# A cross-attention and mixture-of-experts layer in fp32: the first tiles of two experts moved into the seam between the stages, and keys and values projected as three fp32r products of parts

## The chip, the core and the metric

The kernel runs on one core of a Trainium2 chip. The metric is the device time of one execution in microseconds (us), from the first to the last instruction of the core and what lies around it. Three runs of the kernel before took 1197.14, 1199.79 and 1202.40 us, a median of 1199.79 us. The execution that was profiled took 1202.42 us, of which the trace's span is 1200.6 us.

## The reference

There are 16 batches of 256 tokens with 256 features, 16 heads of 16 features in the attention, and 8 experts with an inner width of 1024, of which each token goes to 2.

```python
x = x + tanh(g_xattn) * attention(layernorm(x), ctx, ctx)     # 16 heads, projections with biases
h = layernorm(x)
bids = sigmoid(h @ conf_w.T + conf_b) * wealth                # 8 experts
top_bids, selected = top_k(bids, 2)
combine = one_hot(selected) * softmax(top_bids)
x = x + tanh(g_ffn) * sum_e combine_e * (silu(h @ gate_e.T) * (h @ up_e.T)) @ down_e.T
```

The wealth of the experts differs, so the routing is skewed. With the inputs that are timed, the experts receive 1, 1, 272, 1, 3820, 1, 3 and 4093 of the 8192 assignments.

## The kernel before

The kernel has two stages, each written out engine by engine, with semaphores between the engines. Every engine executes its own list in order: SyncE (SP) and GpSimd (POOL) issue the DMAs, TensorE (PE) multiplies and transposes, ScalarE (ACT) and VectorE (DVE) read the PSUM results.

**The attention stage** (`attention_stage`) handles one batch after another. An iteration, the function `body` of each engine, holds work of several batches at once: the scores and the weighted values of batch b (`score`, `weigh`), the values and the row maxima of batch b+1 (`project_v`, `max_scores`), the layer norm and the projections of queries and keys for batch b+2 (`norm_x`, `project_k`, `project_q`), the output projection and the second layer norm of batch b-1, and the routing of batch b-2 (`first_choice`, `second_choice`, `positions`, `scatter`). The scatter writes each token's normalized row, with its weights and its number, to the region of each chosen expert in a DRAM tensor, `dispatched`. Batches 2 to 13 run in a hardware loop of two iterations a turn; iterations 0, 1, 14 and 15 are written out.

In an iteration GpSimd executes this list: the four small operations of the layer norm's scale for batch b+2 (`scale_x`, L1069 to L1072), the split of the dense keys into a rounded part and a rest (`split`, L1089 and L1091), the scale of the second layer norm, the split of the queries, four indirect DMAs (`scatter`, L1098), and the addition of the output bias to x (`add_bias`, L1081). ScalarE begins an iteration with `norm_x` of batch b+2, which waits for `scale_x`, and executes the exponentials of batch b (L703) behind it. TensorE's second `score` of the iteration writes the PSUM tile that the first exponential must have read. Keys and values are projected by plain fp32 matmuls of the context and the weights (L463 and L478).

**The seam.** After iteration 15 the last batch goes through a chain with one engine after another: heads turned, output projection, residual and second layer norm, routing, scatter. Then the rows behind each expert's last row are padded (`pad_experts`, from SP's and ACT's queues). All engines wait in `attention_over` until everything has landed. Only then are the rows of expert 0 loaded (`load_rows`, L1248). The weights of expert 0 are loaded at the start of the kernel, those of experts 1 and 2 behind `attention_over` (L87).

**The expert stage** (`expert_stage`) goes through the experts 0 to 7. The first tile of each has 128 rows and is computed in fp32 (`first`: gate and up at L1330, transposes at L1341, down at L1350). It is computed for every expert, whatever its count. Meanwhile ScalarE and VectorE split the expert's weights into a rounded fp32r part and a rest. Tiles behind it have 256 rows and consist of fp32r products of parts (`rest`, L1287 to L1301). Their number is read from the counts: 1 for expert 2, 15 for expert 4, 16 for expert 7, none for the others. Each tile's result is added to the output by indirect DMAs (L1511, L1519).

Of the kernel before, what the change touches and what calls it, by code (L numbers as in the profile page):

```python
# [21 lines left out]
P = 128  # L22
# [14 lines left out]
STAGES = 3  # L37
ROW = 272
COMB = D
# [18 lines left out]
def build_program(nc, x, ctxT, wq, wk, wv, wo, bq, bk, bv, bo, confT, conf_b, wealth, g_attn, g_ffn,  # L58
# [3 lines left out]
    with ExitStack() as keep:  # L62
# [8 lines left out]
        stage = sb(keep, "stage", [P, WCOLS])  # L71
# [3 lines left out]
        tiles = sb(keep, "tiles", [P, EXPERTS], i32)  # L75

# [3 lines left out]
        s_padded = [sem("expert0_padded"), sem("others_padded")]  # L80
# [3 lines left out]
        def load_third(eng, e, n, to):  # L84

            of = (gate_T, up_T, down_T)[n][e]
            eng.dma_start(to[:, n * third:(n + 1) * third], of).then_inc(s_stage[e % STAGES][n], 16)  # L87

        *attention, attention_over = attention_stage(nc, sb, sem, load_third, stage, disp, out, x, ctxT, wq, wk, wv, wo,
                        bq, bk, bv, bo, confT, conf_b, wealth, g_attn, g_ffn, ident, tri,  # L90
                        expert_row, expert_no, token_no, ones_at, pick_rows, pad_rows, idn, pads, s_padded, counts, tiles)
        experts = expert_stage(nc, sb, sem, load_third, disp, out, idn, tiles, stage, s_stage, s_hi, s_split, s_padded, attention_over)
        block = keep.enter_context(nc.Block())

        @block.sync
        def _(sp):
            attention[0](sp)
            experts[0](sp)

        @block.tensor  # L100
        def _(pe):
            attention[1](pe)
            experts[1](pe)

        @block.scalar
        def _(act):
            attention[2](act)
            experts[2](act)

        @block.vector  # L110
        def _(dve):
            attention[3](dve)
            experts[3](dve)

        @block.gpsimd
        def _(pool):
            attention[4](pool)
            experts[4](pool)
# [18 lines left out]
def attention_stage(nc, sb_in, sem, load_third, stage, disp, out, x, ctxT, wq, wk, wv, wo,  # L137
                    bq, bk, bv, bo, confT, conf_b, wealth, g_attn, g_ffn, ident, tri,
                    expert_row, expert_no, token_no, ones_at, pick_rows, pad_rows, idn, pads, s_padded, counts, tiles):
    with ExitStack() as own:  # L140
# [3 lines left out]
        x_all = sb("x_all", [P, BATCHES, QT, D])  # L144
# [3 lines left out]
        wv_s = sb("wv_s", [P, HC, D])  # L148
        wo_s = sb("wo_s", [P, HC, D])
        bq_s = sb("bq_s", [P, HC])  # L150
# [23 lines left out]
        xn = sb("xn", [P, QT, D])  # L174
        xT = sb("xT", [P, HC, SEQ])
        dense = {what: sb(f"{what}_dense", [P, HC, SEQ]) for what in "QK"}
        high = {what: sb(f"{what}_high", [P, HC, SEQ], f32r) for what in "QK"}
        rest = {what: sb(f"{what}_rest", [P, HC, SEQ], f32r) for what in "QK"}
        q = [sb(f"queries{i}", [P, HPAIRS, SEQ], f32r) for i in range(2)]
        k = [sb(f"keys{i}", [P, HPAIRS, SEQ], f32r) for i in range(2)]  # L180

        picks = {what: sb(f"picks_{what}", [P, QT, P], f32r) for what in ("Q high", "Q rest", "K high", "K rest")}
# [4 lines left out]
        probs = [sb(f"probs{i}", [P, HPG, QT, SEQ]) for i in range(2)]  # L187
# [25 lines left out]
        w2 = sb("w2", [P, QT])  # L213
# [1394 lines left out]
```

## Time and profile before

| what | us |
|---|---|
| median of three runs | 1199.79 (1197.14 to 1202.40) |
| the profiled execution | 1202.42 |
| its span | 1200.6 |
| before the steady iterations of the attention | 0 to 102.5 |
| iterations 2 to 13 | 102.5 to 431.0 |
| iterations 14 and 15 | 431.0 to 476.6 |
| the seam, to the first matmul of expert 0 | 476.6 to 514.7 |
| first tiles of experts 0 and 1 | 514.7 to 542.3 |
| the rest of the experts | 542.3 to 1200.6 |

In a row of the timeline stand the start, the duration, the engine, the line, the operation, the output and its inputs, and in brackets how long the engine had been idle before it and what ended that. An fp32 matmul shows as two records. TensorE's granted clock (PEclk) is given as a share of 2.4 GHz; it is either 1.00 or 0.50, and a value between them is a mean over a stretch that had both. Busy time of TensorE includes the modelled ends of its matmuls.

### The profile page before, as it was taken

To read this page: it belongs to the slowest core of one execution; us is meant where nothing else is said; L and a number is where in the kernel's file an instruction comes from. 1 tells how busy PE (TensorE), PEld (TensorE's weight loads), DVE (VectorE), ACT (ScalarE), POOL (GpSimd) and SP (SyncE) were. 2 spreads that over 40 slices of the span, in tenths; PEclk is the share of its full clock that TensorE was granted. 3 is DMA by queue.
4 is the path that set the end of the run, shared out by engine and by line. 5 is a ranking of instruction groups with operands and counts; after the bars stand their busy time and mean duration, and the time that the engine had idled before them with its cause. 6 is when DMAs were issued, how large, how long until landed. Compare 5 with 4: busy or idle time off the path is not lost. (4 is left out here: it accounts for less than half of the span.)

```text
span 1200.6 us, 24032 instructions
## 1 busy us (share of the span) xinstructions
PE 1091.6 (91%) x8213; PEld 896.2 (75%) x8213; DVE 668.0 (56%) x1588; ACT 555.3 (46%) x891; POOL 315.6 (26%) x366
## 2 busy tenths in 40 slices
PE   5789999999999988289899999999989999999994
PEld 4456666666666655247599999999849999999994
DVE  2546777777777774365644444444564444444442
ACT  3456676666676664155533333333453333333331
POOL 2122444444343332311311122112221122112111
PEclk8899999999999997589999999999999999999998
DMA  8100111111111101384621121112141122112111
GB/s 297 52 15 24 39 37 44 48 46 37 37 37 37 44 30 48 121 317 164 220 56 32 22 36 32 28 30 36 31 140 28 22 36 36 31 23 36 32 26 23
DMA packets 48025, 72.85 MB, mean 61 GB/s; under 512 B 6256, under 2 KB 42864, under 8 KB 44912
## 3 DMA queue, kind: packets, MB, share of 16 engines
q0 software_dynamic: 16896, 43.53, 14.2%
q1 hardware_dynamic: 30000, 27.68, 7.8%
q10 hardware_dynamic: 1088, 1.11, 0.3%
q8 instruction: 23, 0.38, 0.1%
q14 instruction: 18, 0.15, 0.0%
HBM read 47.14 MB, written 24.90 MB: 60 GB/s over the span
## 5 line engine op out<-in xcount | busy, mean ns | idle before, releaser
L1519 POOL DMA_INDIRECT out<-y,token x64 | 104.6, 1634 | 473.1 <-DVE y L1453 364.1
L1379 ACT ACTIVATE silu<-gate 128x512 f32<-128x512 f32 x128 | 76.5, 597 | 277.4 <-PE up L1287 277.4
L1299 PE MATMUL down<-w_split,h_hi 128*128 128x512 f32 x512 | 185.9, 398 | 0.0
L901 DVE TENSOR_REDUCE max_neg<-maxps 128x4 f32<-128x1024 f32 x128 | 156.4, 1222 | 52.8 <-PE maxps L510 51.1
L1287 PE MATMUL gate<-x_hi,w_split 128*128 128x256 f32 x1024 | 184.5, 282 | 0.0
L1287 PE MATMUL up<-x_hi,w_split 128*128 128x256 f32 x1024 | 183.8, 281 | 0.0
L1444 DVE TENSOR_TENSOR h<-silu,up 128x512 f32<-128x512 f32 x128 | 88.0, 688 | 171.4 <-ACT silu L1379 171.4
L703 ACT ACTIVATE probs<-scores 128x1024 f32<-128x1024 f32 x124 | 127.8, 1030 | 60.5 <-PE scores L535 60.5
L1287 PEld LDWEIGHTS gate<-x_hi,w_split 128*128 128x128 f32 x1024 | 148.8, 188 | 3.0
L1287 PEld LDWEIGHTS up<-x_hi,w_split 128*128 128x128 f32 x1024 | 147.8, 188 | 0.0
L1301 PE MATMUL down<-w_split,h_lo 128*128 128x256 f32 x512 | 144.2, 282 | 0.0
L1446 DVE TENSOR_TENSOR h_lo<-h,h_hi 128x512 fp32r<-128x512 f32 x128 | 88.6, 692 | 89.3 <-ACT h_hi L1382 89.3
L1382 ACT ACTIVATE h_hi<-h 128x512 fp32r<-128x512 f32 x128 | 80.8, 632 | 96.5 <-DVE h L1444 96.5
L1299 PEld LDWEIGHTS down<-w_split,h_hi 128*128 128x128 f32 x512 | 96.3, 188 | 17.4
L1287 PE MATMUL up<-x_lo,w_split 128*128 128x256 f32 x512 | 102.8, 282 | 0.0
L1287 PE MATMUL gate<-x_lo,w_split 128*128 128x256 f32 x512 | 102.6, 282 | 0.0
L1301 PEld LDWEIGHTS down<-w_split,h_lo 128*128 128x128 f32 x512 | 96.6, 189 | 0.0
L1287 PEld LDWEIGHTS up<-x_lo,w_split 128*128 128x128 f32 x512 | 78.7, 189 | 0.0
L1287 PEld LDWEIGHTS gate<-x_lo,w_split 128*128 128x128 f32 x512 | 78.0, 188 | 0.0
L546 PE MATMUL pv<-probs,values 128*32 128x256 f32 x1024 | 71.1, 397 | 1.4 <-ACT probs L703 1.4
L535 PE MATMUL scores<-queries,keys 64*128 64x256 f32 x496 | 60.0, 321 | 12.6 <-ACT probs L703 9.0
L510 PE MATMUL maxps<-keys,queries 48*128 48x256 f32 x512 | 60.8, 316 | 11.1 <-DVE max_neg L901 8.9
(164 smaller groups left out, 1756.3 us busy)
## 6 DMA issues: line engine op xcount, KB each, us to landing
xg<-dispatched SPq DMA_DIRECT2D x41, 272.0 KB, 2.8
stage<-gate_T POOLq DMA_DIRECT2D x8, 1024.0 KB, 7.5
stage<-up_T POOLq DMA_DIRECT2D x8, 1024.0 KB, 9.4
stage<-down_T POOLq DMA_DIRECT2D x8, 1024.0 KB, 12.0
x_all<-x SPq DMA_DIRECT2D x16, 256.0 KB, 6.3
ctxT<-ctxT SPq DMA_DIRECT2D x16, 256.0 KB, 2.7
out<-x_all SPq DMA_DIRECT2D x16, 256.0 KB, 2.1
out<-y,token POOLq DMA_INDIRECT x72, 3.8
```

Of the source, the lines that this page charges most:

```text
L510: last = mm(maxps[:, u, t, :], q[par][r, pair, t * P:(t + 1) * P], k[par][r, pair, :], start=True, stop=True)
L546: last = mm(pv[j * SLOT:(j + 1) * SLOT, 0:SEQ], v[par][:, t, g * HPG + j, :], probs[g % 2][:, j, t, :], start=t == 0, stop=t == QT - 1)
L703: nc.scalar.activation(probs[g % 2][:, at:at + HPP].rearrange("p u t s -> p (u t) s"), home(b, pair), ACT.Exp).then_inc(s["unit_read"], 1)
L901: V.tensor_reduce(to, maxps[:], AX.X, ALU.max, negate=True).then_inc(s["max_taken"], 1)
L1287: last = mm(bank[:, i, :], weights(w, mat)[:, c, cols], r[:, c, :], start=m == 0, stop=m == len(terms) - 1)
L1299: mm(down[t][:].rearrange("p (n d) -> p n d", n=2), h_hi[:, i, rows], split[:, :, cols], start=i == 0, stop=False, skip_group_check=True)
L1301: last = mm(down[t][:, 0:D], h_lo[:, i, rows], hi[:, cols], start=False, stop=i == IC - 1, skip_group_check=True)
L1379: nc.scalar.activation(silu[pair % 2][:], gate[pair % 2][:], ACT.Silu).then_inc(s_silu, 1)
L1382: nc.scalar.activation(h_hi[:, 2 * pair:2 * pair + 2, :], h[pair % 2][:], ACT.Copy).then_inc(s_hhi, 1)
L1444: V.tensor_tensor(h[pair % 2][:], silu[pair % 2][:], up[pair % 2][:], ALU.mult).then_inc(s_made, 1)
L1446: V.tensor_tensor(h_lo[:, 2 * pair:2 * pair + 2, :], h[pair % 2][:], h_hi[:, 2 * pair:2 * pair + 2, :].bitcast(fp32), ALU.subtract).then_i ...
L1519: pool.indirect_dma_start(out, bass.IndirectOffsetOnAxis(token[:, t:t + 1], axis=0), y[:, t, :], None, compute_op=ALU.add).then_inc(s_adde ...
```

## The change

The change has four parts.

**Parts of keys and values.** From iteration 2 on, the keys of batch b+2 and the values of batch b+1 are projected by `project_k_in_parts` and `project_v_in_parts`: the context and the weights are each split into a rounded fp32r part and a rest, and three of the four products of parts are summed, 12 fp32r matmuls in place of 4 fp32 ones. VectorE splits the weights once, before iteration 0 (`split_weights`); TensorE waits for it before iteration 0. GpSimd splits the context of batch b+3 at the end of each iteration (`split_ctx`), twice in iteration 1.

**Early tiles.** The first tiles of experts 0 and 1 are computed in the seam, interleaved with the last batch's chain on TensorE, ScalarE and VectorE. Their rows come from batches 0 to 12 alone. Where an expert has under 128 rows by then, as both have here, its later rows are placed behind row 128 (`space_early_experts`), and zero rows stand between; these are stored from SP's queue before iteration 0, and GpSimd waits for them there (`first_rows_padded`). The main loop then runs over experts 2 to 7, and last over tiles of experts 0 and 1 behind the first, of which there are none with these inputs.

**Loads.** The weights of expert 1 are loaded during the attention into a buffer of their own, those of expert 2 ahead of the last batch's scatter, those of experts 3 and 4 behind it. Weights of experts 0 and 1 are loaded once more in the main loop.

**Pads.** Those of experts 0 to 3 are stored from SP's queue, those of 4 to 7 from GpSimd's, behind the last scatter. Experts 4 to 7 are waited for only ahead of expert 4's rows.

```diff
+            def project_k_in_parts(b, par, use):
+                pe.wait_ge(s["ctx_split"], b - 2)
+                use.free(pe, "K")
+                terms = three_terms(w_high["k"], w_rest["k"], c_high[par], c_rest[par])
+                for o in range(HC):
+                    for n, (l, r, c) in enumerate(terms):
+                        last = mm(use.bank("K")[:, o, :], l[:, c, o * P:(o + 1) * P], r[:, c, :], start=n == 0, stop=n == len(terms) - 1)
+                last.then_inc(s["misc_written"], 1)
...
+            def split_ctx(c, par, use):
+
+                alone.wait_ge(s["ctx_loaded"], c * 16 + 16)
+                use.written(alone, "V")
+                G.tensor_copy(c_high[par][:], cT[par][:]).then_inc(s["ctx_high_made"], 1)
+                alone.wait_ge(s["ctx_high_made"], c - 2)
+                G.tensor_tensor(c_rest[par][:], cT[par][:], c_high[par][:].bitcast(fp32), ALU.subtract).then_inc(s["ctx_split"], 1)
...
                     scatter(b - 2, par)
                 if ahead:
                     add_bias(b + 2)
+                if isinstance(b, int) and b == 1:
+                    split_ctx(3, 1, use)
+                if ahead and not is_first(b):
+                    split_ctx(b + 3, 1 - par, use)
...
             add_bias(0)
             add_bias(1)
+            pool.wait_ge(s["first_rows_padded"], 16 * EARLY)
...
+                if pair >= 6:
+                    split_weights(pair - 6, "kv"[pair - 6], (wk_s, wv_s)[pair - 6])
             read_maxima(0, PRO1)
...
             sp.dma_start(out[TOKENS:], pads[:, 0:D]).then_inc(s["pads_stored"], 16)
+            for e in range(EARLY):
+                sp.dma_start(disp[e * REGION:e * REGION + FIRST], pads[:]).then_inc(s["first_rows_padded"], 16)
...
+            turn_last_heads()
+            pe.wait_ge(s["unit_read"], handed["units"])
+            turn_rows(16 * EARLY, EARLY)
+            turn_last_normed()
+            early_product(0, 0, 0)
+            project_last_out()
+            early_product(0, 0, 1)
+            early_product(0, 1, 0)
+            early_product(0, 1, 1)
+            turn_last_x2()
+            early_flip(0, 0)
+            last_logits()
...
+            scatter_next_to_last()
+            pool.wait_ge(s["x2_stored"], 16 * BATCHES)
+            load_weights(EARLY)
+            scatter_last()
...
+        ORDER = [*range(EARLY, EXPERTS), *range(EARLY)]
```

GpSimd's list around the end of an iteration in the loop, before. `rstd` and `shift` are the four operations of `scale_x` for the next iteration; the rows named ISA set registers for waits.

```order
L1098 DMA dispatched<-row,posi 34816x272 x4
L1081 ISA
L1081 TENSOR_TENSOR x_all<-x_all,bo_s 128x512
L131 ISA
L1069 TENSOR_SCALAR rstd<-mv 128x2
L131 ISA
L1070 TENSOR_TENSOR rstd<-rstd,minus_half 128x2
```

And GpSimd's list at the same place now.

```order
L1183 DMA dispatched<-row,posi 34816x272 x4
L1158 ISA
L1158 TENSOR_TENSOR x_all<-x_all,bo_s 128x512
L131 ISA x2
L1164 CAST ctx_high<-ctxT 128x512
L131 ISA
L1166 TENSOR_TENSOR ctx_rest<-ctxT,ctx_high 128x512
L131 ISA
L1146 TENSOR_SCALAR rstd<-mv 128x2
L131 ISA
L1147 TENSOR_TENSOR rstd<-rstd,minus_half 128x2
```

The two operations of `split_ctx` stand between the bias and the scale on which the next iteration's first instruction of ScalarE waits.

TensorE's list in the seam before, from the transposes of the last heads (L556) to the count (L691) and the first rows of expert 0 (L1276).

```order
L556 MATMUL misc<-idn,oS 128x128 x8
L451 MATMUL misc<-idn,on 128x128 x4
L568 MATMUL misc<-wo_s,oT 128x256 x4
L588 MATMUL misc<-m,before 128x8
L591 MATMUL misc<-macc,ones 128x8
L588 MATMUL misc<-m,before 128x8
L590 MATMUL misc<-m,ones 128x8
L591 MATMUL misc<-macc,ones 128x8
L451 MATMUL misc<-idn,row 128x128 x4
L580 MATMUL misc<-conf_s,x2T 128x8 x4
```

And TensorE's list now, from the same transposes to the logits (L614). `x_early` holds the turned rows of experts 0 and 1.

```order
L590 MATMUL misc<-idn,oS 128x128 x8
L1399 MATMUL turned<-idn,xg 128x128 x4
L464 MATMUL misc<-idn,on 128x128 x4
L1498 MATMUL gate<-stage,x_early 128x512 x2
L602 MATMUL misc<-wo_s,oT 128x256 x4
L622 MATMUL misc<-m,before 128x8
L625 MATMUL misc<-macc,ones 128x8
L622 MATMUL misc<-m,before 128x8
L624 MATMUL misc<-m,ones 128x8
L625 MATMUL misc<-macc,ones 128x8
L1498 MATMUL up<-stage,x_early 128x512 x2
L1498 MATMUL gate<-stage,x_early 128x512 x2
```

Two matmuls of expert 0's tile stand ahead of the last output projection, and six more stand between the ranks and the transposes of the last normalized rows. The other matmuls of the two tiles follow in the same way, between the logits and the first rows of expert 2.

## Rows read from the trace of the kernel before

**Rows 1.** Stretches: length, busy time (instructions) of five engines, granted clock, DMA, GB/s.

```profile
102.50:431.00 328.50, 306.17 (x2728) 214.23 (x2724) 245.80 (x684) 221.34 (x348) 140.40 (x204) 1.00 0.12 40
476.60:514.70 38.10, 10.50 (x39) 8.39 (x39) 13.26 (x80) 6.02 (x12) 12.52 (x19) 0.58 0.40 141
514.70:542.30 27.60, 26.89 (x88) 15.27 (x88) 18.97 (x27) 17.69 (x26) 3.32 (x4) 0.90 0.80 317
```

**Rows 2.** Timeline of TensorE, a steady iteration: second scores, keys, second scores.

```profile
327.94 0.50 PE L535 MATMUL scores<-queries,keys 64*128 64x256 f32 x4
...
353.38 1.99 PE L463 MATMUL misc<-ctxT,wk_s 128*128 128x256 f32 x8
355.31 0.50 PE L535 MATMUL scores<-queries,keys 64*128 64x256 f32 x4
```

**Rows 3.** Timeline of TensorE, fp32r matmuls of 256 columns in a 256-row tile.

```profile
562.42 0.64 PE L1287 MATMUL up<-x_hi,w_split 128*128 128x256 f32 x4
562.89 0.40 PE L1287 MATMUL up<-x_lo,w_split 128*128 128x256 f32 x2
```

**Rows 4.** Timeline of GpSimd, from the split of the queries to the next scale.

```profile
341.64 0.61 POOL L1089 CAST Q_high<-Q_dense 128x512 fp32r<-128x512 f32 x1 [1.87 <-ACT Q_dense L739]
342.40 1.28 POOL L1091 TENSOR_TENSOR Q_rest<-Q_dense,Q_high 128x512 fp32r<-128x512 f32 x1 [0.15 <-POOL Q_high L1089]
...
348.76 1.28 POOL L1081 TENSOR_TENSOR x_all<-x_all,bo_s 128x512 f32 x1
350.27 0.23 POOL L1069 TENSOR_SCALAR rstd<-mv 128x2 f32<-128x2 f32 x1 [0.23 <-DVE mv L859]
```

**Rows 5.** Timeline of ScalarE, the start of the same iteration.

```profile
352.22 1.09 ACT L717 ACTIVATE xn<-x_all,shift,rstd 128x256 f32 x2 [2.11 <-POOL shift L1072]
353.22 1.00 ACT L703 ACTIVATE probs<-scores 128x1024 f32<-128x1024 f32 x1
```

**Rows 6.** Stretches as in rows 1: around falls of the clock, and a steady one.

```profile
445.00:452.00 7.00, 4.12 (x48) 2.59 (x52) 5.59 (x22) 5.19 (x8) 3.64 (x7) 0.98 0.14 50
588.60:592.00 3.40, 3.40 (x6) 1.35 (x5) 1.92 (x2) 0.00 (x0) 3.05 (x4) 0.55 1.02 429
325.80:332.70 6.90, 6.35 (x58) 4.48 (x57) 5.81 (x13) 5.76 (x11) 1.88 (x2) 1.00 0.00 0
```

**Rows 7.** Timeline of iteration 0, and GpSimd's at the start of iteration 2.

```profile
47.23 0.43 SPq L419 DMA_DIRECT2D out<-pads  x1
...
47.00 0.23 POOL L1069 TENSOR_SCALAR rstd<-mv 128x2 f32<-128x2 f32 x1 [18.53 <-DVE mv L859]
...
49.87 1.00 ACT L703 ACTIVATE probs<-scores 128x1024 f32<-128x1024 f32 x1
...
52.94 0.50 PE L535 MATMUL scores<-queries,keys 64*128 64x256 f32 x4
...
104.10 0.22 POOL L1069 TENSOR_SCALAR rstd<-mv 128x2 f32<-128x2 f32 x1 [5.83 <-DVE mv L859]
```

**Rows 8.** Timeline of the seam and the first tiles of experts 0 to 2.

```profile
478.88 3.68 PE L568 MATMUL misc<-wo_s,oT 128*128 128x256 f32 x8 [0.69 <-ACT oT L731]
...
487.94 1.11 PE L451 MATMUL misc<-idn,row 128*128 128x128 f32 x4 [4.92 <-ACT row L726]
...
495.63 1.28 ACT L833 ACT_TABLE_LOAD   x1
...
503.29 0.96 POOL L1098 DMA_INDIRECT dispatched<-row,posi  x1 [0.30 <-issue]
...
509.14 0.06 DVE L1479 MEMSET note<- 128x4 f32 x1 [9.38 <-DMA dispatched<-row,posi]
...
514.73 3.78 PE L1330 MATMUL gate<-stage,x_full 128*128 128x512 f32 x4 [1.69 <-DVE x_lo L1419]
...
529.91 1.96 PE L1330 MATMUL gate<-stage,x_full 128*128 128x512 f32 x4
...
542.40 1.89 PE L1330 MATMUL gate<-stage,x_full 128*128 128x512 f32 x4
```

More of the change, by code:

```diff
@@ L67, in sem @@
             return keep.enter_context(nc.semaphore(name))
-        stage = sb(keep, "stage", [P, WCOLS])
+        stage = [sb(keep, f"stage{i}", [P, WCOLS]) for i in range(EARLY)]
         idn = sb(keep, "idn", [P, P])
@@ L1186, in expert_stage @@
         s_first_added = sem("first_added")
+        s_own_hi = [sem(f"expert{e}_weights_hi") for e in range(EARLY)]
+        s_own_split = [[sem(f"expert{e}_weights_split{n}") for n in range(3)] for e in range(EARLY)]
         third = WCOLS // 3
@@ L1365, in first, with early_product @@
                 first_contract(e, 1, range(IC // 2)).then_inc(s_down, 1)
-            turn_rows(16)
+            def early_product(e, half, mat):
+                if mat == 0 and half == 0:
+                    pe.wait_ge(s_xhi, EARLY)
+                    for n in range(2):
+                        wait_stage(pe, e, n)
+                for c in range(HC):
+                    last = mm(early_bank((gate, up)[mat], e, half)[:].rearrange("p a b -> p (a b)"),
+                              x_early[:, c, e * FIRST:(e + 1) * FIRST],
+                              weights(stages[e], mat)[:, c, half * (INNER // 2):(half + 1) * (INNER // 2)],
+                              start=c == 0, stop=c == HC - 1)
+                if mat == 1:
+                    last.then_inc(s_pair, 2)
@@ new lines, in early_flip @@
+            def early_flip(e, half):
+                pe.wait_ge(s_made, e * PAIRS + (2 * half + 4))
+                if half == 1:
+                    pe.wait_ge(s_flipped, 2 * e + 1)
+                for i in range(IC // 2):
+                    last = nc.tensor.transpose(early_bank(gate, e, 0)[:].rearrange("p a b -> p (a b)")[:, i * P:(i + 1) * P],
+                                               h[half][:].rearrange("p a b -> p (a b)")[:, i * P:(i + 1) * P], idn[:])
+                last.then_inc(s_flip, 1)
@@ new lines, in early_contract @@
+            def early_contract(e, half, pieces):
+                wait_stage(pe, e, 2)
+                pe.wait_ge(s_flipped, 2 * e + half + 1)
+                w = weights(stages[e], 2)
+                for i in pieces:
+                    at = half * (IC // 2) + i
+                    last = mm(early_bank(up, e, 0)[:].rearrange("p a b -> p (a b)")[:, 0:D], hT[half][:, i, :], w[:, at, :],
+                              start=at == 0, stop=at == IC - 1)
+                return last
+            turn_last_heads()
@@ L1383, in rest, with round_part, before_rest @@
                 high_of_rows(n + 2)
+            def round_part(e, m, half, done):
+                wait_stage(act, e, m)
+                nc.scalar.activation(hi[:, part(m, half)], stages[e % STAGES][:, part(m, half)], ACT.Copy).then_inc(done, 1)
+            def before_rest(e, r):
+                if e < EARLY:
+                    act.wait_ge(s_down, r + EXPERTS)
+                    for m in range(3):
+                        act.wait_ge(s_split[m], 2 * splits_before(EXPERTS))
+                    for m, half in HALVES:
+                        round_part(e + EXPERTS, m, half, s_own_hi[e])
             def first(e, r, n):
@@ L1387, in round_weights @@
                     for m, half in halves:
[L1388 to L1389 removed]
+                        round_part(e, m, half, s_hi)
                 def first_silu(half):
```

466 lines of the change are left out of this document (307 added, 159 removed).

## Prediction

> **What bounds the kernel now.** I first cut the span into its stages [rows 1]. In the twelve steady iterations of the attention TensorE is busy for 306 of 328.5 us, in the first tiles of two experts for 26.9 of 27.6 us. In the seam it is busy for 10.5 of 38.1 us, at a mean clock of 0.58, while the last batch goes from engine to engine. So TensorE sets the time in the stages, and a chain of waits in the seam. Next I read the timeline where the change puts instructions. The second scores of an iteration come 27.37 us after those of the one before [rows 2]. Beside TensorE runs a second chain that is almost as long: GpSimd splits the queries, issues four scatters, adds the bias, computes the scale; then ScalarE normalizes x and does the first exponential, which TensorE's second scores wait for [rows 4, 5]. How much air that chain has decides what the first part of the change is worth.
>
> **Keys and values in parts.** The fp32 projection holds TensorE for 1.93 us, from 353.38 to 355.31 [rows 2]; values have the same shapes. An fp32r matmul of 256 columns takes 0.118 us, four of them 0.47 us from 562.42 to 562.89 [rows 3]; twelve take 1.42 us. Each projection gives back 0.5 us. There are 12 of keys and 13 of values; if TensorE alone decided, the gain would be 12.5 us.
>
> It does not decide. The split of a batch's context on GpSimd has the shapes of the split of the queries: 0.61 + 0.15 + 1.28 us, with the registers for its waits about 2.15 us [rows 4]. It stands between the bias and the scale. The air in front of the scale is 0.23 us (it waits for VectorE until 350.27) [rows 4]. The first exponential ends at 354.22 [rows 5], and TensorE's second scores start at 355.31 [rows 2], 1.09 us later, of which 0.06 us is the signal. Together that is 1.26 us of air, and 2.15 us is put in: the second scores come 0.9 us later than before. From there to the next projection of queries, and through GpSimd's list to the next scale, each step waits for the one before, and nothing in it gets shorter: both projections that do lie ahead of the second scores, where TensorE will now wait. So the iteration grows to 28.3 us, and the 1.0 us that it saves becomes part of a wait of 1.9 us. This holds at 11 starts of iterations (3 to 13): +9.9 us. At the start of iteration 2 GpSimd was idle for 5.83 us [rows 7], which holds both of its splits; iterations 2 and 14 therefore keep what they save, three projections, -1.5 us. Bounds for this term: -12.5 us (no wait) and 11 x 2.15 = +24 us (no air).
>
> VectorE's instructions may be held up while GpSimd computes. The splits fall beside VectorE's reading of the values; even 2 us there would be hidden, since TensorE waits for the exponential anyway. I take nothing.
>
> **The clock in these iterations.** TensorE's clock fell after 445 to 452, where it was busy for 4.12 of 7.00 us; in a steady iteration it was busy for 6.35 of 6.90 us around the second scores and stayed at 2.4 GHz [rows 6]. With the new wait (1.9 us, of which 0.16 us is covered by the modelled end of the last matmul) that place has 4.6 of 6.9 us. This is much nearer to the row that fell. I take a fall at every second of the 11 places. A fall costs at least half of a stretch like 588.6 to 592.0, 1.7 us [rows 6]: 5.5 x 1.7 = +9 us. Bounds: 0, and 11 falls of twice that length, +37 us.
>
> The Trainium skill (TensorE: Matmul & The Clock Gate, "Why this matters for your kernels") names only long idle gaps between bursts of matmuls as what brings the clock down. By that rule waits of 1.9 us would leave it up, the 9 us would be 0, and this is the first rival. The trace does not agree with it in full: in 445 to 452, before the fall, TensorE had no such gap and was busy for 4.12 of 7.00 us [rows 6].
>
> **Ahead of iteration 0.** GpSimd's scale of batch 2 starts at 47.00 [rows 7]. Now it waits for two stores of zero rows that SP issues behind `out<-pads`, at 47.23 [rows 7] and later by what the split of the weights on VectorE puts in front of the last maxima: a copy and a subtraction, about 1.2 us (GpSimd takes 1.28 us for such a subtraction alone [rows 4]). With the issue of two stores more and about 2 us to land (an estimate) this is 51.5, so +4.5 us. The first exponential ended at 50.87, and the second scores of iteration 0 started at 52.94 [rows 7], 2 us later; +2.6 us remain. Bounds 0 and +5.
>
> **The seam.** A first tile takes 12.49 us at 2.4 GHz, from 529.91 to 542.40 [rows 8]; two take 25 us. TensorE is idle in the seam for 27.6 us [rows 1], and its own 10.5 us get shorter when the clock stays up. The pieces stand where the chain is elsewhere. Two matmuls (1.7 us) go ahead of the output projection, which took 3.68 us while the clock fell [rows 8] and takes 2.0 us with it up; this is even. Six matmuls (5.2 us) fit into the 4.92 us before 487.94 [rows 8], since the projection ends sooner. ScalarE loads its table again ahead of the sigmoid and of the next silu; 1.28 us each [rows 8], of which about 0.6 us comes onto the chain. I expect the last scatter within 1 us of 503.29. It stands on GpSimd's queue behind 3.1 MB of expert 2's weights; at the 317 GB/s of 514.7 to 542.3 [rows 1] these take 10 us from about 493, so they end with the scatters. Half of the pads are no longer ahead of it all. So expert 2 starts where expert 0 did, at 514.73, in place of 542.40: -27.7 us. It also takes over expert 0's low clock, 15.2 us (514.73 to 529.91) in place of 12.5: +2.7 us. For the four late pads I take -1 us. Sum -26 us. Bounds: 0 (all of it at 1.2 GHz, 50 us of tiles in 38 us of seam) and -29.
>
> **The end.** Reading the two counts of experts 0 and 1 again, +0.5 us. Their second loads of weights, 6.3 MB, lie beside the 31 large tiles of experts 4 and 7: nothing. If that cover were gone, the rate above would make it 20 us.
>
> **The sum.** -1.5 + 9.9 + 9 + 2.6 - 26 + 0.5 = -5.5 us, so 1202.42 becomes 1196.9 for an execution like the profiled one. That one lies 2.6 us above the median of the three; against the median it is 1194.3, and I forecast 1194 us.
>
> **The rivals.**
> 1. *The clock stays up in the attention.* For it: 4.6 of 6.9 us is still a larger share than that of the stretch that fell. Against it: it is nearer to that one than to the steady one. The 9 us fall away: 1185 us.
> 2. *GpSimd's chain has more air than I count*, for instance because its list runs ahead, and TensorE keeps the 12.5 us. Then the sum is -12.5 + 2.6 - 26 + 0.5 = -35.4: 1164 us. Against it: the idle 2.11 us of ScalarE before it normalizes x show that it already waits for GpSimd [rows 5].
> 3. *The clock falls in nearly every iteration* (slower). The place is the wait ahead of the second scores; the price is 1.7 us for each fall and 3.4 us where the clock stays down for twice as long. Without falls the sum is -14.5 us, so it decides from 14.5 us on, nine single falls in eleven. With eleven falls of mean 2.6 us it is +29 - 14.5 = +14: 1214 us.
> 4. *The seam gives nothing back:* the clock is low through it as before, or the last scatter waits behind the weights. Then 20 of the 26 us are lost: 1214 us. For it: mean clock 0.58 now [rows 1]. Against it: TensorE is nearly always busy there afterwards.
>
> **How the numbers follow.** The forecast has 0.41, with its own range from 1187 to 1202; rival 1 has 0.17, rival 2 0.10, rival 3 0.17, rival 4 0.15. About 0.5%, 6 us, is what a measurement of this kernel can tell from no change. Faster than 1193.8: rivals 1 and 2, and under half of the forecast (0.18): 0.45. Slower than 1205.8: most of rivals 3 and 4: 0.28. Between them 0.27. The range from 1176 to 1213 leaves out rival 2 and the far half of 3 and 4.
>
> **What would show it.** The second scores 28.3 us apart, with GpSimd's context split directly before the scale and ScalarE waiting about 4 us for the scale; TensorE waiting about 1.8 us for the first exponential; stretches of clock 0.50 between 110 and 440. Expert 2's first matmul near 515 plus what came before. Wrong would be: a period under 27.4 us; no wait for the exponential; TensorE still busy with expert 1 when expert 2's rows have landed.

## The result, and the profile after

| | kernel before | changed kernel |
|---|---|---|
| median of its timed runs | 1201.25 us (1196.91 to 1204.61, 16 runs) | 1204.52 us (1200.85 to 1212.16, 16 runs) |
| span of the profiled execution | 1200.6 us | 1201.2 us |
| ratio | 1 | 1.0041, 95% interval 1.0023 to 1.0059 |

The change made the kernel 0.4% slower (medians 3.3 us apart); the forecast was 1194 us, 5.5 us less than before. Follow one instruction per place through both traces, and one sees where the difference arises. "Rest of the keys" is GpSimd's subtraction `K_rest` (L1091 before, L1176 now), which stands in each of the iterations 0 to 13:

| place | before | after | difference so far |
|---|---|---|---|
| rest of the keys, iteration 3 | 139.73 | 139.90 | +0.2 |
| rest of the keys, iteration 13 | 413.43 | 421.79 | +8.4 |
| expert 2's first matmul | 542.40 | 536.10 | -6.3 |
| expert 4's first matmul | 587.82 | 582.49 | -5.3 |
| end of the span | 1200.6 | 1201.2 | +0.6 |

So the attention lost 8.4 us, the seam gave back 14.7 us where 26 were forecast, experts 2 and 3 lost 1.0 us, and from expert 4's first tile on 5.9 us were lost, of which the prediction had 0.5 us. These are differences of two single executions: the one profiled before lies 1.2 us above its kernel's median, the one after 1.6 us below.

The stretches of the profile after (columns as in [rows 1]); the second row holds the new seam with the tiles of experts 0 and 1, the third what follows them:

```profile
102.50:431.00 328.50, 292.23 (x2734) 210.24 (x2734) 241.48 (x678) 214.33 (x337) 154.78 (x220) 1.00 0.12 42
478.00:517.20 39.20, 35.23 (x191) 22.12 (x183) 18.51 (x106) 17.36 (x29) 20.96 (x29) 1.00 0.53 189
517.20:537.00 19.80, 2.03 (x6) 1.21 (x6) 2.32 (x5) 2.85 (x5) 5.00 (x8) 0.60 0.99 365
```

The granted clock is 1.00 throughout the steady iterations, and also in the seam, where it was 0.58 [rows 1]. There TensorE is now busy for 35.23 of 39.20 us. But then it is busy for only 2.03 of 19.80 us, while the DMA engines are busy throughout (0.99).

The end of a steady iteration on GpSimd, ScalarE and TensorE, which answers to [rows 2, 4, 5]:

```profile
275.40 1.09 ACT L771 ACTIVATE xn<-x_all,shift,rstd 128x256 f32 x2 [3.97 <-POOL shift L1149]
...
299.52 0.61 POOL L1164 CAST ctx_high<-ctxT 128x512 fp32r<-128x512 f32 x1
300.28 1.28 POOL L1166 TENSOR_TENSOR ctx_rest<-ctxT,ctx_high 128x512 fp32r<-128x512 f32 x1
301.64 0.23 POOL L1146 TENSOR_SCALAR rstd<-mv 128x2 f32<-128x2 f32 x1
...
305.65 0.50 PE L569 MATMUL scores<-queries,keys 64*128 64x256 f32 x4 [1.35 <-ACT probs L757]
```

The scale of x directly follows the split of the context, with no idle time left ahead of it (0.23 us before). ScalarE waits 3.97 us for it (2.11 before), and TensorE 1.35 us for the first exponential. The period, that is the time from one iteration to the next, read at the rest of the keys from iteration 3 to 13, is 28.19 us (27.37 before).

The seam after on GpSimd, SP and TensorE:

```profile
500.83 0.60 POOL L91 DMA_DIRECT2D stage<-gate_T  x1
...
510.77 0.96 POOL L1183 DMA_INDIRECT dispatched<-row,posi  x1 [0.30 <-issue]
511.73 2.24 POOL L373 DMA_DIRECT2D dispatched<-pads  x3
...
516.67 1.25 POOL L91 DMA_DIRECT2D stage<-gate_T  x1
...
522.88 13.70 SPq L1365 DMA_DIRECT2D xg<-dispatched  x2
...
533.03 1.08 PE L1399 MATMUL turned<-idn,xg 128*128 128x128 f32 x4 [15.78 <-DMA xg<-dispatched]
536.10 3.75 PE L1456 MATMUL gate<-stage,x_full 128*128 128x512 f32 x4 [1.99 <-DVE x_lo L1644]
```

Two transfers are late. SP may issue expert 2's rows only when the last scatter has landed; that is at 522.88, 11.2 us after its issue ended (before: 509.11, 4.9 us). And TensorE turns (transposes) these rows, 272 KB, only 10.15 us after that (before 2.8 us, 509.11 to 511.93). It had been done with expert 1's tile since 517.25.

The large tiles, grouped, first before and then after (columns: count | busy us, mean ns of one):

```profile
L1299 PE MATMUL down<-w_split,h_hi 128*128 128x512 f32 x512 | 185.9, 398 | 0.0
L1287 PE MATMUL gate<-x_hi,w_split 128*128 128x256 f32 x1024 | 184.5, 282 | 0.0
```

```profile
L1422 PE MATMUL down<-w_split,h_hi 128*128 128x512 f32 x512 | 187.3, 403 | 0.0
L1410 PE MATMUL gate<-x_hi,w_split 128*128 128x256 f32 x1024 | 186.1, 284 | 0.0
```

The matmuls of both groups are a little slower at the same clock. From the turning of one tile's rows to the next it is 17.59 us and not 17.41; 31 times this is 5.6 us, nearly all of the 5.9.

### The profile page after: what moved, and what is told of

Read it like the earlier page. It is cut to its first block and busy times, and to the rows that moved or that the text cites. A ratio compares the mean times of both kernels' runs of the same rounds, so it can differ in the third digit from the quotient of the medians.

```text
span 1201.2 us, 24318 instructions
## 1 busy us (share of the span) xinstructions
PE 1083.5 (90%) x8310; PEld 897.7 (75%) x8310; DVE 654.5 (54%) x1575; ACT 545.3 (45%) x877; POOL 346.2 (29%) x404
## 5 line engine op out<-in xcount | busy, mean ns | idle before, releaser
L1410 PEld LDWEIGHTS up<-x_hi,w_split 128*128 128x128 f32 x1024 | 150.3, 191 | 0.0
L569 PEld LDWEIGHTS scores<-queries,keys 64*128 64x128 f32 x496 | 38.1, 189 | 58.2 <-ACT probs L757 36.3
```

Of the source, the lines that this page charges most:

```text
L569: last = mm(to[:, u * QT + t, :], k[par][r, pair, t * P:(t + 1) * P], q[par][r, pair, :], start=True, stop=True)
L1410: last = mm(bank[:, i, :], weights(w, mat)[:, c, cols], r[:, c, :], start=m == 0, stop=m == len(terms) - 1)
```

## The experiments

All ratios are against the kernel before, with 95% intervals; a time is the median of that kernel.

### The slower large tiles: e1, e5, e6, e10

e1 is the kernel before with the tiles of the experts where the changed kernel has them:

```diff
-        stages = [stage] + [sb(f"stage{i}", [P, WCOLS]) for i in range(1, STAGES)]
-        split = sb("w_split", [P, 2, WCOLS], f32r)
         xg = sb("xg", [P, TT, ROW])
+        x_early = sb("x_early", [P, HC, EARLY * FIRST])
...
+        h_hi = sb("h_hi", [P, IC, TILE], f32r)
+        split = sb("w_split", [P, 2, WCOLS], f32r)
+        h_lo = sb("h_lo", [P, IC, TILE], f32r)
```

> The kernel before with nothing changed but where the experts' tiles (rows, weights, their parts) lie in SBUF: the places of the changed kernel. Theory: the 256-row tiles of the changed kernel take 17.60 us and not 17.41 because of these places, so here their period becomes 17.60 and the time rises by 31 x 0.18 = 5.7 us, to about 1207. Rival: the slower tiles come from what the changed kernel does beside them (the second loads of weights, other instruction addresses, the power of what ran before); then the period stays 17.41 and the time 1201.

1206.06 us, ratio 1.0058 (1.0040 to 1.0076); from one large tile to the next 17.59 us. Its groups are those of the changed kernel:

```profile
L1303 PE MATMUL down<-w_split,h_hi 128*128 128x512 f32 x512 | 187.3, 403 | 0.0
L1291 PE MATMUL gate<-x_hi,w_split 128*128 128x256 f32 x1024 | 186.1, 284 | 0.0
```

So the places alone make the tiles as slow, without any work beside them. The next three keep the order of before and only insert unused gaps:

```diff
+        gap0 = sb("gap0", [P, 320])
         split = sb("w_split", [P, 2, WCOLS], f32r)
...
+        gap1 = sb("gap1", [P, 480])
         x_hi = sb("x_hi", [P, HC, TILE], f32r)
...
+        gap2 = sb("gap2", [P, 256])
         h_hi = sb("h_hi", [P, IC, TILE], f32r)
```

This is e5, with gaps of 320, 480 and 256 elements of 4 bytes; e6 has 96, 480 and 256, e10 only the first gap of 320. e11 to e16, further down, bring the changed kernel's tiles back to 17.41 us by such gaps.

> The kernel before with three unused gaps in the experts' SBUF, so that the parts of the weights, of the rows and of the hidden values start at the same remainder of 2048 bytes (896) as in the changed kernel (before: 1664, 1792 and 768), the order of the tiles being that of before. Theory: the slower large tile (17.60 us against 17.41) comes from these remainders; then the period is 17.60 and the time about 1206. Rival: it comes from the order, that is from the region of SBUF in which the parts lie; then the period stays 17.41 and the time 1201.

> The same gaps with other sizes, so that the parts of the weights, rows and hidden values all start at a multiple of 2048 bytes. If remainders matter, the period is another than 17.41 us, and an even start is at least as good as before: 17.2 to 17.4. If only the region matters, it stays 17.41 and the time 1201.

> The kernel before with one unused gap of 1280 bytes ahead of the parts of the weights: all parts move together, weights from remainder 1664 to 896 of 2048 (as in the changed kernel), rows from 1792 to 1024, hidden values from 768 to 0. Theory A: what counts is the distance of the two operands of a matmul (in both slow kernels weights, rows and hidden values had the same remainder); the distances stay as before, so 17.41 us and 1201. Theory B: the weights' own remainder counts: 17.60 us and 1206.

| | start in bytes, remainder of 2048: weights, rows, hidden | from tile to tile, us | time, ratio |
|---|---|---|---|
| before | 1664, 1792, 768 | 17.41 | 1 |
| e5 | 896, 896, 896 | 17.59 | 1208.02 us, 1.0070 (1.0054 to 1.0086) |
| e6 | 0, 0, 0 | 17.61 and 17.54 in turn | 1205.68 us, 1.0048 (1.0033 to 1.0062) |
| e10 | 896, 1024, 0 | 17.41 | 1200.46 us, 0.9999 (0.9985 to 1.0013) |

The order of the tiles does not matter (e5), and round addresses do not help, contrary to what I expected of e6. e10 has the weights at the remainder of the slow kernels and is fast. In every slow kernel the two operands of a matmul start at the same remainder, and in no fast one. Why this costs time stays open. Distances other than these were not tried, nor whether 2048 is the size that counts.

### The split of the context on GpSimd: e2, e3, e9, e12

e2 has no parts: keys and values in fp32, no split on GpSimd.

```diff
-                if isinstance(b, int) and b < 2:
+                if nxt:
                     project_v(1 - par, use)
-                elif nxt:
-                    project_v_in_parts(b + 1, 1 - par, use)
...
-                if ahead and not is_first(b):
-                    split_ctx(b + 3, 1 - par, use)
```

> The changed kernel with keys and values projected in fp32 as before; no context is split on GpSimd. Theory: the period of 28.19 us comes from that split alone, so it goes back to 27.37 and the seam starts 8 us earlier: about 1196. Rival: part of the 8.4 us comes from the new order of the first iterations or from the new places in SBUF; then the second scores are still more than 27.6 us apart, and the time stays over 1200.

1194.63 us, 0.9957 (0.9940 to 0.9974); period 27.38. So the 28.19 us come from the parts and their split together. That it is the place of the split, e3 shows, where only that place changes:

```diff
                     split(b + 2, "K", use, units_before(b) + (UNITS.index("K1") + 1 - len(UNITS)))
+                if ahead and not is_first(b):
+                    split_ctx(b + 3, 1 - par, use)
                 if back:
                     scale_of(b - 1, "scale2_chain", "ln2_stats", mv2, rstd2, shift2, "ln2_scaled")
```

> The changed kernel with the split of the context moved in GpSimd's list from behind the bias to behind the split of the keys, where GpSimd idles about 5 us before the scale of the second norm. Theory: the chain through GpSimd is as long as before (27.37 less its air of 1.26 = 26.1 us) and TensorE decides: 27.37 - 1.0 = 26.4 us a period, 1.8 us less than 28.19 in 11 of them, about 1185. Rival: the split now stands beside VectorE's long instructions and delays its statistics of the second norm, or another wait of TensorE takes over: a period of 27 us or more and 1192 or more.

1197.86 us, 0.9974 (0.9952 to 0.9996): a miss for the theory. The period is 27.35 and not 26.4. GpSimd's, VectorE's and TensorE's rows, in e3:

```profile
278.91 1.26 POOL L1166 TENSOR_TENSOR ctx_rest<-ctxT,ctx_high 128x512 fp32r<-128x512 f32 x1
...
279.51 0.70 DVE L988 SCALAR_TENSOR_TENSOR bids<-m,bids 128x16 f32<-128x16 f32 x1
...
281.57 0.27 PE L622 MATMUL misc<-m,before 128*128 128x8 f32 x1 [0.94 <-DVE m L995]
```

An instruction of VectorE on 16 elements took 0.70 us (0.17 in the changed kernel), until GpSimd's subtraction was over; the masks came as much later, and TensorE waited 0.94 us for them instead of 0.42. The second reason is TensorE's own saving. The first two rows and the matmul behind the values, in e3:

```profile
267.76 0.50 PE L512 MATMUL misc<-wv_high,ctx_high 128*128 128x256 f32 x2
268.11 0.40 PE L512 MATMUL misc<-wv_rest,ctx_high 128*128 128x256 f32 x2
...
269.38 0.50 PE L544 MATMUL maxps<-keys,queries 48*128 48x256 f32 x4
```

The values took 1.62 us (267.76 to 269.38) and the keys 1.68 us, against 1.92 us each: 0.54 us an iteration and not 1.0. The first pair of a projection in parts takes 0.35 us and the last 0.33 (values) or 0.38 (keys), where the others take 0.24. Saving and new wait cancel.

The Trainium skill (SBUF — State Buffer, "SBUF: two separate sides") says that a GpSimd instruction that reads the SBUF and a VectorE instruction with two SBUF inputs cannot run at once: the second is blocked for the whole length of the first. The trace agrees, here (0.70 us) and in e9 (1.23 us). The prediction had this effect and took nothing for it, because it looked only at VectorE's reading of the values.

Two more places for the same two lines: e9 ahead of the split of the queries, e12 ahead of the split of the keys.

> The changed kernel with the context split between GpSimd's scale of the second norm and its split of the queries, where it idles 1.9 us. With the split behind that of the keys the period was 27.33 us: the two projections in parts saved 0.54 us (1.62 + 1.68 us in place of twice 1.92), and TensorE waited 0.52 us longer for the second choice's masks, one instruction of which took 0.70 us on VectorE in place of 0.17 while GpSimd subtracted. Theory: that is all that decides; here the masks are ready before the subtraction, TensorE keeps the 0.54 us, GpSimd's chain grows by only 0.3 us of its 1.26: period 26.83, 13 to 16 us less than the changed kernel, about 1190. Rival: another link of VectorE (the positions, the maxima) is held up and TensorE waits there: period 27.3 or more, 1196 or more.

1219.47 us, 1.0154 (1.0130 to 1.0178). My theory failed and the rival was right, by more than it said. GpSimd, VectorE and TensorE in e9 (its profiled execution took 1229.91 us, the longest of its six):

```profile
301.45 1.30 POOL L1166 TENSOR_TENSOR ctx_rest<-ctxT,ctx_high 128x512 fp32r<-128x512 f32 x1 [0.15 <-POOL ctx_high L1164]
...
301.56 1.23 DVE L1022 TENSOR_TENSOR t<-m,w 128x16 f32<-128x16 f32 x1
302.71 0.63 DVE L1023 TENSOR_TENSOR c<-m,w 128x16 f32<-128x16 f32 x1
...
304.84 0.50 PE L544 MATMUL maxps<-keys,queries 48*128 48x256 f32 x4 [1.93 <-DVE max_neg L958]
...
308.25 1.93 PE L580 MATMUL pv<-probs,values 128*32 128x256 f32 x16
```

The positions of the rows are small VectorE instructions with two SBUF inputs, and the maxima that TensorE waits for are queued behind them. Every second iteration now takes 29.7 to 36.3 us and the others about 28.2, the longer ones with falls of the granted clock: behind the wait of 1.93 us the sixteen matmuls of a product with the values take 1.93 us, where they take 1.07 us in the changed kernel. The mean clock of 110 to 170 is 0.83. In every iteration there is one such wait, of 1.65 to 1.94 us, and none of TensorE's waits is longer.

> The changed kernel with the context split between GpSimd's scale of x and its split of the keys, where it idles 4.8 us. Theory: what counts is which instructions of VectorE fall beside the subtraction (1.3 us); here they are the maxima and the second half of the heads, of which TensorE's transposes wait with about 0.5 us to spare. So the masks are on time (wait 0.42 us), TensorE keeps the 0.54 us and the period is 26.83: about 1189. Rival: the maxima or the heads come late instead and TensorE waits for them, 27.4 us or more: 1197 or more.

1190.08 us, 0.9916 (0.9893 to 0.9938), period 26.78. Beside the subtraction now stand VectorE instructions that take one of their inputs from the PSUM and are no longer for it (0.42 us, as in the changed kernel). The masks are on time, and TensorE keeps what it saves:

```profile
272.24 1.30 POOL L1166 TENSOR_TENSOR ctx_rest<-ctxT,ctx_high 128x512 fp32r<-128x512 f32 x1 [0.15 <-POOL ctx_high L1164]
...
273.37 0.42 DVE L920 TENSOR_TENSOR on<-misc,rsum 128x256 f32<-128x256 f32 x1
...
280.98 0.27 PE L622 MATMUL misc<-m,before 128*128 128x8 f32 x1 [0.38 <-DVE m L995]
```

The same two instructions in four places of one list thus give 28.19, 27.35, 28.2 to 36 and 26.78 us. GpSimd idled long enough for them in two of the four, and one of these two gave nothing.

### The seam: e4, e7, e8

In e4 the weights of expert 2 are issued behind the last scatter:

```diff
-            load_weights(EARLY)
             scatter_last()
+            load_weights(EARLY)
```

> The changed kernel with the load of expert 2's weights (3.1 MB) issued behind the last scatter and the pads instead of ahead of the scatter. Theory: the rows of the last batch landed late because they stand on one queue behind the weights; now SP may load expert 2's rows about 5 us after the last scatter, near 517 instead of 522.9, and expert 2's first matmul comes near 527 instead of 536: 1196. Rival: the late landing comes from the pads or from all 16 DMA engines being busy; then SP still waits until about 522, or the weights themselves now come last, and expert 2 starts at 536 or later: 1204 or more.

1202.12 us, 1.0016 (1.0003 to 1.0030). The cause of the late scatter was right, and the gain in time was not. SP, GpSimd and TensorE in e4:

```profile
514.52 0.96 POOL L1183 DMA_INDIRECT dispatched<-row,posi  x1 [0.30 <-issue]
...
518.65 0.56 POOL L91 DMA_DIRECT2D stage<-gate_T  x1
...
519.50 17.15 SPq L1365 DMA_DIRECT2D xg<-dispatched  x2
...
533.07 1.09 PE L1399 MATMUL turned<-idn,xg 128*128 128x128 f32 x4 [11.96 <-DMA xg<-dispatched]
```

With nothing ahead of it on the queue the last scatter lands 4.0 us after its issue and not 11.2. But expert 2's weights are now issued 0.85 us ahead of its rows, and the rows take 13.6 us. e7 leaves that order and holds the other loads back:

```diff
-            pool.wait_ge(s_down, 1)
+            pool.wait_ge(s_turned, EARLY + 1)
             load_weights(EARLY + 1)
```

> The changed kernel in which GpSimd issues the loads of the weights of experts 3 and 4 only when expert 2's rows have been turned. Theory: these rows (272 KB) take 10 us to land because 3 to 6 MB of weights are in flight; alone they take about 3 us, SP issues them at 522.9 as before, and expert 2's first matmul comes near 529 instead of 536: 1197.5. Rival: the rows are late for another reason (what is still queued from the scatters and the pads), or expert 3's weights now come late; then TensorE still turns them near 533, or waits before expert 3: 1204.

1201.71 us, 1.0016 (0.9998 to 1.0034). SP and TensorE in e7:

```profile
524.71 0.38 SPq L1365 DMA_DIRECT2D xg<-dispatched  x1
...
527.69 1.09 PE L1399 MATMUL turned<-idn,xg 128*128 128x128 f32 x4 [6.66 <-DMA xg<-dispatched]
...
549.09 0.50 PE L1410 MATMUL gate<-x_hi,w_split 128*128 128x256 f32 x2 [3.08 <-DVE x_lo L1644]
```

The rows are issued at 524.71 and turned 3.0 us later. In expert 2's second tile TensorE then waits 3.08 us, where the changed kernel shows no wait. e8 does both, with only gate and up ahead of the scatter, and puts the pads of experts 4 to 7 last:

```diff
-            load_weights(EARLY)
+            for n in range(2):
+                load_third(pool, EARLY, n, stages[EARLY])
             scatter_last()
...
-            pool.wait_ge(s_down, 1)
+            pool.wait_ge(s_turned, EARLY + 1)
+            load_third(pool, EARLY, 2, stages[EARLY])
             load_weights(EARLY + 1)
             pool.wait_ge(s_added, 16)
             pool.wait_ge(s_down, 2)
-            load_weights(EARLY + 2)
             add_early(1, s_first_added)
+            load_weights(EARLY + 2)
+            pad_high()
```

> The changed kernel with both late landings in the seam taken away: ahead of the last scatter only gate and up of expert 2's weights (2 MB), the loads of its down weights and of experts 3 and 4 behind the turning of its rows, the pads of experts 4 to 7 behind all of them. Theory: the last rows land about 5 us after their scatter, SP loads expert 2's rows near 516, they land by 520, and expert 2 starts near 523 instead of 536: 13 us less than 1204.5, about 1191.5. Rival: gate and up still lie ahead of the last rows on the queue, or expert 1's own tile (until 517.4) and the weights for down come last; then it starts at 528 or later: over 1196.

1191.21 us, 0.9922 (0.9908 to 0.9937), as its theory had it. SP issues the rows 3.9 us after the last scatter's issue, although 2 MB of weights still stand ahead of that scatter, and TensorE waits 1.44 us:

```profile
517.57 6.29 SPq L1367 DMA_DIRECT2D xg<-dispatched  x2
...
520.65 0.63 PE L1401 MATMUL turned<-idn,xg 128*128 128x128 f32 x4 [1.44 <-DMA xg<-dispatched]
523.26 3.16 PE L1458 MATMUL gate<-stage,x_full 128*128 128x512 f32 x4 [1.99 <-DVE x_lo L1646]
```

The traces enter the seam at other times, so compare the way from expert 0's first matmul to expert 2's: 48.7 us in the changed kernel (487.44 to 536.10), 44.9 in e4, 39.5 in e7, 33.9 in e8. Clearing the queue alone gives 3.8 us of this way, holding the loads back alone 9.1, and both 14.8. But e7 gives half of its gain away again: from expert 2's first matmul to expert 4's it takes 51.1 us, the changed kernel 46.4. What the moved pads of e8 are worth was not tried by itself.

### All of it: e11, e13, e14, e15, e16

These have the seam of e8, four gaps that give weights, rows and hidden values the remainders of the kernel before, and GpSimd's wait for the zero rows in iteration 1 instead of ahead of iteration 0. They differ in the split of the context: at e9's place (e11), no parts (e13), at e3's place (e14), at e12's (e15). e16 is e15 with SP's stores of zero rows behind batch 2's context:

```diff
                     load_ctx(b + 2, par)
+                    if b == 0:
+                        sp.wait_ge(s["pads_loaded"], 16)
+                        sp.dma_start(out[TOKENS:], pads[:, 0:D]).then_inc(s["pads_stored"], 16)
```

> The changed kernel with all of it mended: seam as in the seam experiment (13 us), the parts of weights, rows and hidden values at the remainders of the kernel before by four unused gaps (31 x 0.18 = 5.6 us), the context split ahead of the split of the queries (12 x 1.36 = 16 us if the period is 26.83, 10 if it is 27.33), and the wait for the two stores of zero rows moved from ahead of iteration 0 to iteration 1 (2.4 us). Theory: the terms add up, 1204.5 - 37 = 1167, or 1173 with the longer period. Rival: what one place gives back another takes (the weights of expert 2 or the last rows come relatively later, the clock falls in the shorter seam): over 1180.

> No parts (keys and values in fp32), with the seam of e8, the operands at the remainders of the kernel before, and the wait for the zero rows in iteration 1. Theory: the terms add up: 1194.6 (seam experiment without parts) less 13.3 for the seam, 5.6 for the offsets and 1.1 for the wait = 1174.6. Rival: the seam gives less when the rest moves: over 1180.

> As e13, but with keys and values in parts, the context split behind the keys' split (period 27.33 us). Theory: there the parts are worth nothing in the steady iterations (27.33 against 27.37) and 1 us in the first ones, so 1173 to 1175, within 0.3% of e13. Rival: the parts are worth 5 us or more once nothing else hides them: 1169.

> As e14, with the context split ahead of the keys' split. Theory: period 26.83, 6 us less than e14: 1168. Rival: period 27.4 or more, as slow as e14 or slower.

> As e15, with SP's three stores of zero rows issued behind the load of batch 2's context instead of ahead of it. Theory: in e15 TensorE waits for that context once GpSimd no longer waits for the stores; here the first split of keys comes about 2 us earlier, near 56.5 instead of 58.8, and the time is 2 us less: 1168. Rival: the low clock of TensorE in these stretches decides and the split stays at 58.5: 1170.

| | period of an iteration | time | ratio |
|---|---|---|---|
| e11 | 28.2 and 29.9 in turn | 1204.71 us | 1.0043 (1.0019 to 1.0066) |
| e13 | 27.38 | 1176.36 us | 0.9803 (0.9778 to 0.9829) |
| e14 | 27.35 | 1180.19 us | 0.9833 (0.9804 to 0.9862) |
| e15 | 26.78 | 1170.03 us | 0.9757 (0.9733 to 0.9780) |
| e16 | 26.80 | 1173.81 us | 0.9786 (0.9761 to 0.9812) |

e11 missed, for e9's reason; its large tiles are at 17.41 us. e15 is the fastest: 2.4% below the kernel before. The terms add up: 1204.5 less 14.4 (e12), 13.3 (e8) and 5.6 (the places) is 1171.2, and 1170.0 was measured. For e13, 1194.6 less 13.3 and 5.6 is 1175.7, measured 1176.4. e14 missed its 1175; from e3's median the same sum is 1179.0. These sums have nothing for the moved wait for the zero rows; what it is worth no run shows by itself.

Ahead of iteration 0 one wait hid another. In e14 GpSimd's scale is back at 47.01, but the keys' rest still comes at 58.61, and TensorE waits for the context behind SP's stores:

```profile
52.12 2.50 PE L476 MATMUL misc<-ctxT,wk_s 128*128 128x256 f32 x5 [0.92 <-DMA ctxT<-ctxT]
```

In e16 that rest comes at 56.56 (58.77 in e15), as its theory has it. At iteration 13 only 0.8 us of this is left (405.61 against 406.42), and the time does not fall: its median is higher than e15's, and the intervals overlap. Its profiled execution also lost time far behind this place: TensorE waited 2.52 us ahead of expert 7's first matmul (0.27 us in e15), and from the turning of expert 7's first rows to that of its next rows it took 16.86 us (12.92 in e15, 11.78 in the changed kernel, 17.17 in e8). Single executions thus differ by 4 to 5 us at this one place, and the six runs of e16 do not settle which of the two is faster.

## Why the prediction was wrong

- **The second scores 0.9 us later at 11 starts (+9.9).** Right: +0.82 us an iteration, 8.2 us from iteration 3 to 13, and ScalarE's wait of 3.97 us. Taking the parts and their split away (e2) takes it away, and so does moving the split (e3, e12). What I never asked is where else in GpSimd's list the split could stand.
- **The saving of a projection (0.5 us).** Mis-sized by a factor of two: 0.30 for the values, 0.24 for the keys (e3). I took twelve matmuls at the pace of a long row of equal ones; the first and the last pair each take about 0.1 us more. In the steady iterations it was covered by the wait, so it hardly touched the sum; it only made the wait 1.35 us (0.54 saved and 0.82 later) and not 1.9.
- **The clock falls in every second iteration (+9).** Wrong: the clock is 1.00 from 102.5 to 431; the first rival's mechanism came true. The wait is 1.35 us, and TensorE is busy for 5.55 of the 6.90 us around the second scores (299.2 to 306.1), where I had 4.6. e9 shows the fall that I had feared, behind waits of 1.65 to 1.94 us. The Trainium skill (TensorE: Matmul & The Clock Gate, "Why this matters for your kernels") names there only long gaps as what brings the clock down. That agrees with the changed kernel; in e9 the clock falls with no single gap over 1.94 us.
- **Ahead of iteration 0 (+2.6).** Right at the place: GpSimd's scale started at 50.21, the second scores of iteration 0 came at 55.05 and not 52.94, and the rest of the keys 2.40 us later. That only 0.2 us is left by iteration 3 is in the main luck of the profiled execution. To the rest of the keys of iteration 1 it took 26.56 us where the trace before took 28.61, and between 60 and 75 the granted clock was 1.00 where it had been 0.80 (first before, then after):

```profile
60.00:75.00 15.00, 12.70 (x112) 8.07 (x114) 5.62 (x9) 8.07 (x11) 3.43 (x5) 0.80 0.01 2
60.00:75.00 15.00, 11.03 (x122) 7.14 (x122) 7.42 (x10) 9.66 (x13) 4.07 (x6) 1.00 0.17 60
```

e4, e7 and e8 have the same attention as the changed kernel. There the clock of that stretch was 0.89, 0.84 and 0.78, the same way took 27.62, 28.86 and 28.74 us, and the rest of the keys of iteration 3 came at 141.35, 142.82 and 140.81, not at 139.90. In the kernel before and the four runs with its attention (e1, e5, e6, e10) it came at 139.12 to 139.73. So the place was 0.2 us later in the profiled execution and 1.1 to 3.7 us later in three others (with 0.8 us of the split already in it). The low clock goes with the longer way in all of them; whether the change makes it fall more often there stays open. The step to iteration 2 took 26.53 us where it had been 27.53, and 27.13 without parts (e2): the parts save 0.6 us there, and the forecast had 1.0 (of its -1.5).
- **The seam (-26).** This is the step that failed. Its working of the tiles was good: e8 has TensorE waiting 1.44 us for the rows, and an expert 2 that starts 33.9 us after expert 0; 514.73 plus the shift of 8.4 us would have made it 35.7 in the changed kernel. What failed are two sentences on transfers, both in the way between the last scatter and expert 2's first matmul. "They end with the scatters": the weights were issued at 500.83 and not near 493, because GpSimd's scatter of batch 14 stands ahead of them, and the last scatter landed 11.2 us after its issue. And expert 2's own rows, which I left as before, now met the loads of experts 3 and 4, which the earlier down matmuls had let go: 10.15 us and not 2.8. This is the second half of rival 4 with a companion that I did not name. e8, with both transfers mended, is 13.3 us faster than the changed kernel.
- **No price at all for the large tiles (+5.6).** The diff moved every tile of the experts in SBUF, and I read that as bookkeeping. It made each of the 32 large tiles 1% longer (e1, e5, e10).
- **The end (+0.5).** Right in size: from the last turned rows to the end of the span it took 20.3 us and not 19.6. That the reading of the counts is what costs them is not shown.

With every term at what the two traces show (the clock 0, the first iterations 0.2, the split's 8.2, the seam and experts 2 and 3 -14.7 + 1.0, the large tiles 5.6, the end 0.8), the sum is +1.1 us, against +0.6 between the traces and +3.3 us between the medians. The forecast missed the medians by 9 us, and luck made this little: the 9 us for the clock, which did not come, covered about half of what the seam and the large tiles cost more than I had.

## What to carry to other kernels

When a change starts a stage earlier, list every DMA that it issues in the order of its queue and ask for each small transfer what stands ahead of it and what flies beside it; the stage starts when that one lands. Work for GpSimd goes where no VectorE instruction with two SBUF inputs leads to a wait of TensorE, and this decides more than how long GpSimd idles there. When buffers are moved or added, compare the mean of a matmul group that the change leaves alone first: a per cent there cost 5.6 us here, over a third of what the seam gave.

## What the runs showed of the hardware

- The start of a matmul's two operands in SBUF changed its pace: 403 ns and 398 for a 512-column matmul, 284 and 282 for one of 256 columns, slow in the four placements in which both start at the same remainder of 2048 bytes (the changed kernel, e1, e5, e6), fast in the two others (before, e10). Whether 2048 is the size that counts no run shows.
- 272 KB in rows of 1088 bytes were turned 2.8 to 3.1 us after their issue with little in flight, and 10.2 and 13.6 us after it with 3 to 6 MB of weights in flight from another queue. The Trainium skill (DMA: Bandwidth & Descriptors, "Queues, rings and completion order") says that a DMA engine takes turns between its queues packet by packet. That small rows beside large ones then get a small share would fit these numbers; no run here shows it by itself.
- A VectorE instruction of 0.17 us took 1.23 us beside a GpSimd subtraction of 1.30 us (e9).
- TensorE's granted clock stayed at 1.00 for 328 us with a wait of 1.35 us in each iteration of 28.19 us (changed kernel), and fell in about every second iteration where each has a wait of 1.65 to 1.94 us (e9).
